# An attention and ternary-FFN kernel: strip 0's scores in the shared buffer, eight of ten transposes moved behind the second score pass

## The chip, the cores and the metric

The kernel runs on all 8 cores of one Trainium2 chip. The batch has 8 sequences, and each core computes one of them by itself with the same program. The metric is the device time of the slowest core in microseconds. One program launch does everything.

## The reference

For each sequence x of 4096 rows by 1024 columns the reference computes two residual layers:

```
x = x + attn(layernorm(x))      # f = ln(x) @ W.T + b
                                # e = f @ f.T + 0.01 * clip(|i - j|, 0, 10)
                                # a = softmax(e, rows) @ f
x = x + ffn(layernorm(x))       # scale = max(mean(|weight|), 1e-5)
                                # ternary = clip(round(weight / scale), -1, 1)
                                # ln(x) @ (ternary * scale).T
```

The score matrix e is 4096 by 4096 for each sequence. Its queries, keys and values are all the same matrix f.

## The kernel before, in words

The 4096 rows are cut into 32 strips of 128. Each engine has a queue of its own, and executes it strictly in the order in which the Python code calls `PR.add`; semaphores join the queues. All instructions of VectorE and ScalarE are recorded at line 114, a helper that wraps each call, so in the trace they are told apart by their tiles.

Phase 1 (strips 0 to 31) loads x, normalizes it, transposes it on TensorE and multiplies by W (L576). The result is `fT`, f transposed, in bf16, for all of the sequence. TensorE also transposes `fT` back into `f`, a strip at a time. The code calls that step "1c": eight 128 by 128 transposes (L481) into one of two PSUM windows `pbt`, and then one copy of 128x1024 out of the window, by VectorE or ScalarE. The two windows alternate, so the third 1c in a row waits until the first has been copied out. Eight of the 32 1c steps are done among the last groups of L576.

The FFN weight is quantized on VectorE. It lies as float32 in eight chunks (0 to 7) in `wstage`, and two instructions turn each chunk into a chunk of `wqT`. `wstage` shares its memory with three buffers of phase 2: chunks 0 to 3 lie where the scores `e` go, chunks 4 and 5 where `pT` goes, and chunks 6 and 7 where `p` goes.

Phase 2 works on one strip of 128 query rows at a time. For strip s, in the program's names:

- `emit_e_mms(s)`: the score pass, 64 matmuls of 128x512 (L723) in eight groups of eight. The groups use four PSUM banks in turn, twice (h = 0, then h = 1). A group of h = 1 waits until the group of h = 0 in its bank has been copied out.
- `emit_e_evacs(s)`: eight copies on ScalarE from PSUM to `e`, and on VectorE the distance bias and eight row maxima, then the maximum of those.
- `emit_exp(s)`: the softmax exponential on ScalarE, from `e` to `p`, with the row sum.
- `emit_A_pack(s, g)`: four packs of eight transposes that turn `p` into `pT`, each with one copy on VectorE. Except for strip 0 they stand inside the score pass of the next strip.
- the A pass: 64 matmuls of 128x512 (L953) that multiply `pT` by `f`, then residual, second layernorm, FFN (L1022) and store.

TensorE's order at the joint of the two phases is: the last L576 groups, the score pass of strip 0, ten 1c steps (`pop_1c(10)`), the score pass of strip 1, the remaining 14 1c steps, the four packs of strip 0, the A pass of strip 0, the score pass of strip 2, and so on. Of the ten 1c steps the 1st, 3rd, 5th, 7th and 9th are copied out by ScalarE, the other five by VectorE; the 14 later ones are all copied out by VectorE.

VectorE's order there is: the quantization of chunks 0 to 3, the row maxima of strip 0, the sum of four partial row sums, the quantization of chunks 4 to 7, the five 1c copies, the 14 1c copies, the four `pT` copies, the row maxima of strip 1. ScalarE's order is: the eight score copies of strip 0, its exponential, the five 1c copies, the eight score copies of strip 1, its exponential.

In the kernel before, strip 0 doesn't use `e` and `p`. Its scores go to four other buffers (`xbuf0`, `xbuf1`, `out1a`, `outbuf`), its exponentials to `lnbuf0`, `lnbuf1`, `ln2` and `ln2T`, in four instructions of 128x1024. So strip 0 doesn't wait for the quantization, and the x loads of the A passes of strips 0 and 1, which go to `xbuf0` and `xbuf1`, wait for its exponential.

Of the kernel before, what the change touches and what calls it, by code (L numbers as in the profile page):

```python
# [8 lines left out]
AF = mybir.ActivationFunctionType  # L9
ALU = mybir.AluOpType  # L10
AXX = mybir.AxisListType.X

P = 128
D = 1024
NH = D // P
# [104 lines left out]
def build_nc(S, sim_mode=False):  # L120
    NST = S // P
    HALF = S // 2
    NSH = NST // 2
    KW = min(512, HALF)
    NKB = HALF // KW
# [69 lines left out]
    with contextlib.ExitStack() as ctx:  # L195
        pb = [ctx.enter_context(nc.psum_tensor(f"pb{i}", [P, 512], F32))
              for i in range(6)]
# [16 lines left out]
        e_sb = view("e", S, F32)  # L214
        pT_sb = view("pT", S, BF16)
        p_sb = view("p", S, BF16)
        xb = [view("xbuf0", D, F32), view("xbuf1", D, F32)]
        lnb = [view("lnbuf0", D, BF16), view("lnbuf1", D, BF16)]
        out1 = [view("out1a", D, F32), view("out1b", D, F32)]
        outb = view("outbuf", D, F32)  # L220
        xb4 = xb + [out1[0], outb]
        sqscr = view("sqscr", D, BF16)
        ln2 = view("ln2", D, BF16)
        ln2T = view("ln2T", D, BF16)
# [3 lines left out]
        stats = view("stats", 48, F32)  # L228
# [6 lines left out]
        LSUM0, LSUM1, RL, SCALE, HTH, NHTH, ABSP, TOT = range(16, 24)  # L235
        PM0 = 24
        NMAX0, NMAX1, ROWI, ROWB = 32, 33, 34, 35
        ABS8 = 40

        def st_(c):  # L240
            return stats[:, c:c + 1]
# [16 lines left out]
        s_vo = mksem("svo")  # L258
# [5 lines left out]
        s_sx = mksem("ssx")  # L264
# [10 lines left out]
        PR = Prog()  # L275
# [127 lines left out]
        def emit_quant_c(c):  # L403
            def v_q(eng, c=c):
                eng.tensor_single_scalar(wqT[:, c * D:(c + 1) * D],
                                         wstage[:, c * D:(c + 1) * D],
                                         st_(NHTH), ALU.is_lt)
                return eng.scalar_tensor_tensor(
                    wqT[:, c * D:(c + 1) * D],
                    wstage[:, c * D:(c + 1) * D], st_(HTH),  # L410
                    wqT[:, c * D:(c + 1) * D], ALU.is_gt, ALU.subtract)
            waits = [(s_ss, wprep["cast_last"])] \
                if not wprep.get("quant_first") else []
            done = PR.add("vector", v_q, waits=waits, inc=s_vq)
            wprep["quant_first"] = True
            if c == 3:
                wprep["quant_e"] = done
            if c == 7:
                wprep["quant_p"] = done
                wprep["quant_last"] = done  # L420

        def x_load(k, waits, nbuf=2):
# [262 lines left out]
            nall += 1  # L685
        f_ready_ve = s_ve.v
        emit_qpre()
        for c in range(4):
            emit_quant_c(c)

        e_evac = {}
# [1 line left out]
        exp_done = {}  # L693
# [37 lines left out]
                        if hc == NH - 1:  # L731
                            e_mm_stop[(s, h, kb)] = v

        e0alt = [xb4[0], xb4[1], out1[0], outb]
        palt = [lnb[0], lnb[1], ln2, ln2T]

        def e_ap(s, bi, r0, r1):
            if s > 0:
                lo = (bi // NKB) * HALF + (bi % NKB) * KW
                return e_sb[:, lo + r0:lo + r1]  # L740
            return e0alt[bi // 2][:, (bi % 2) * KW + r0:(bi % 2) * KW + r1]

        def emit_e_evacs(s):
            c0 = max(s * P - (MAXD - 1), 0)
            c1 = min(s * P + P + MAXD - 1, S)
            for h in range(2):
                for kb in range(NKB):
                    bi = h * NKB + kb
                    lo = h * HALF + kb * KW
                    hi = lo + KW  # L750
                    bc0 = max(lo, c0)
                    bc1 = min(hi, c1)
                    wts = [(s_t, e_mm_stop[(s, h, kb)])]
                    if s > 0 and h == 0 and kb == 0:
                        wts.append((s_sx, exp_done[s - 1]))
                    if s == 1 and h == 0 and kb == 0:
                        wts.append((s_vq, wprep["quant_e"]))

                    def s_ec(eng, s=s, kb=kb, bi=bi):
                        return eng.copy(e_ap(s, bi, 0, KW), pb[kb][:, 0:KW])  # L760
                    got = PR.add("scalar", s_ec, waits=wts, inc=s_ve)
                    assert got == e_evac[(s, h, kb)], "evac reservation"

                    def v_pm(eng, s=s, lo=lo, hi=hi, bc0=bc0, bc1=bc1,
                             bi=bi):
                        if bc1 > bc0:
                            u0 = bc0 - (s * P - (MAXD - 1))
                            eng.tensor_tensor(
                                e_ap(s, bi, bc0 - lo, bc1 - lo),
                                e_ap(s, bi, bc0 - lo, bc1 - lo),  # L770
                                band[:, u0:u0 + (bc1 - bc0)], ALU.add)
                        return eng.reduce_max(st_(PM0 + bi),
                                              e_ap(s, bi, 0, KW), AXX)
                    PR.add("vector", v_pm,
                           waits=[(s_ve, e_evac[(s, h, kb)])], inc=s_vmax)

            def v_max(eng, s=s):
                return eng.reduce_max(st_(NMAX0 + s % 2),
                                      stats[:, PM0:PM0 + 2 * NKB], AXX,
                                      negate=True)  # L780
            max_done[s] = PR.add("vector", v_max, inc=s_vmax)

        def emit_exp(s):
            sc_w = [(s_vmax, max_done[s])]
            if s == 1:
                sc_w.append((s_vq, wprep["quant_p"]))
            if s > 0:
                sc_w.append((s_t, A_done[s - 1]))

            if s == 0:  # L790
                nch = S // D

                def s_exp0(eng):
                    inst = None
                    for j in range(nch):
                        inst = eng.activation(
                            palt[j][:, 0:D], e0alt[j][:, 0:D], AF.Exp,
                            bias=st_(NMAX0), scale=1.0,
                            accum_out=st_(ABS8 + 4 + j))
                    return inst  # L800
                exp_done[s] = PR.add("scalar", s_exp0, waits=sc_w, inc=s_sx)

                def v_lsum(eng):
                    return eng.reduce_sum(st_(LSUM0),
                                          stats[:, ABS8 + 4:ABS8 + 4 + nch],
                                          AXX)
                PR.add("vector", v_lsum, waits=[(s_sx, exp_done[s])],
                       inc=s_vo)
                return

            def s_exp(eng, s=s):
                return eng.activation(p_sb[:, 0:S], e_sb[:, 0:S], AF.Exp,
                                      bias=st_(NMAX0 + s % 2), scale=1.0,
                                      accum_out=st_(LSUM0 + s % 2))
            exp_done[s] = PR.add("scalar", s_exp, waits=sc_w, inc=s_sx)
# [3 lines left out]
        emit_e_mms(0, h_waits=[e0_h0, f_ready_ve])  # L819
        emit_e_evacs(0)  # L820
        emit_exp(0)
        for c in range(4, NH):
            emit_quant_c(c)

        all_1c = c1_half0 + list(range(NSH, NST))
# [2 lines left out]
        def pop_1c(n, eng=None):  # L828
            for _ in range(n):
                if not all_1c:  # L830
                    return
                stt = all_1c.pop(0)
                fw = None
                if stt >= NSH and onec_state[0]:
                    fw = (s_ve, f_ready_ve)
                    onec_state[0] = False
                i = onec_state[1]
                onec_state[1] += 1
                emit_1c(stt, fw, evac_eng=eng or
                        ("scalar" if i % 2 == 0 else "vector"))  # L840

        pop_1c(10)
        f_done = [(s_vp, s_vp.v), (s_sp2, s_sp2.v)]

        NJT = NST
# [5 lines left out]
        for s in range(NST + 1):  # L851
            live = s < NST
            def emit_A_pack(s, g):
                j0 = 8 * g
                n = min(8, NJT - j0)
                if s == 0:
                    srcs = [palt[(j0 + j) // (D // P)][
                        :, ((j0 + j) % (D // P)) * P:
                        ((j0 + j) % (D // P) + 1) * P] for j in range(n)]
                else:  # L860
                    srcs = [p_sb[:, (j0 + j) * P:(j0 + j + 1) * P]
                            for j in range(n)]
                dst = pT_sb[:, j0 * P:(j0 + n) * P]
                transpose_pack(srcs, dst,
                               extra_waits=[(s_sx, exp_done[s])])
                pT_evac[(s, g)] = s_vp.v
# [67 lines left out]
            if live:  # L934
# [31 lines left out]
                    xw = [(s_vln, ln_done[NST - 1])]  # L966
                else:
                    xw = [(s_vo, out1_done[s - 2])]
                if s <= 1:
                    xw.append((s_sx, exp_done[0]))  # L970
                xl = x_load(NST + s, xw)

                out1_nb = {}
# [128 lines left out]
```

How the kernel before makes its waits and increments, by code:

```python
    def emit(self, eng_obj, name, guard_sem=None):  # L52
        guard = None
        if guard_sem is not None:
            guard = _ChainGuard(eng_obj, guard_sem)
            eng_obj = guard
        waited = {}
        for fn, waits, inc, inc_amt, post in self.streams[name]:
            for (s, v) in waits:
                if waited.get(s.name, -1) >= v:
                    continue
                waited[s.name] = v
                eng_obj.wait_ge(s.h, v)
            inst = fn(eng_obj)
            if inc is not None:
                assert inst is not None
                if guard is not None and inc_amt != 16:
                    guard.commit_group(inst, inc, post)
                else:
                    inst.then_inc(inc.h, inc_amt)
# [15 lines left out]
    def _flush_prev(self):  # L86
        if self._prev is not None:
            self._prev.then_inc(self._sem.h, 1)
            self._n += 1
            self._marker = (self._sem.h, self._n)
            self._prev = None
# [1 line left out]
    def commit_group(self, inst, inc, post_val):  # L93
        assert inst is self._prev or self._prev is None
        self._prev = None
        inst.then_inc(inc.h, 1)
        self._marker = (inc.h, post_val)
# [1 line left out]
    def wait_ge(self, *a, **k):  # L99
        return self._eng.wait_ge(*a, **k)
# [9 lines left out]
        def wrap(*a, **k):  # L110
            self._flush_prev()
            if self._marker is not None:
                self._eng.wait_ge(self._marker[0], self._marker[1])
            inst = real(*a, **k)
            self._prev = inst
            return inst
```

## Time and profile before

| what | value |
|---|---|
| median of three runs | 1306.87 us (1306.41 to 1306.93) |
| the profiled execution's own time | 1306.79 us |
| span of its slowest core, core 0 | 1305.0 us |
| spans of the other seven cores | 1300.9 to 1303.0 us |
| TensorE matmul busy | 1247.5 us, 96% |
| VectorE busy | 610.7 us, 47% |
| ScalarE busy | 446.4 us, 34% |
| mean granted TensorE clock, by core | 0.986 to 0.989 |

The span is the time from a core's first to its last instruction. Times in the rows are counted from the span's start. A clock of 1.00 in a row is the full 2.4 GHz of TensorE, 0.50 is 1.2 GHz, and a value between is a mean over the stretch.

### The profile page before, as it was taken

The page shows a single profiled execution, that of the slowest core. Times are in us where ns is not written, and L with a number is a line of the kernel's source. Part 1 is how long each engine was busy: PE and PEld are TensorE (multiplying, and loading weights), DVE is VectorE, ACT ScalarE, POOL GpSimd, SP SyncE. Part 2 cuts the span into 40 slices and gives each one's busy share as a digit, 9 for nine tenths or more (in the row PEclk, how much of TensorE's full clock was granted, in tenths as well). Part 3 has the DMA queues.
Part 4 walks back from the last instruction along what each step waited for, and adds up shares of the span by engine and source line. Part 5 has one row for each costly group of instructions (what it writes and reads, how often), then busy time and mean ns, then how long its engine had stood idle before and what let it go on. Part 6 is the DMA issues. An engine that isn't in the chain of part 4 may idle for free.

```text
span 1305.0 us, 19556 instructions; the slowest of 8 cores (1300.9 to 1305.0 us)
## 1 busy us (share of the span) xinstructions
PE 1247.5 (96%) x7100; PEld 632.2 (48%) x7100; DVE 610.7 (47%) x945; ACT 446.4 (34%) x670; POOL 12.6 (1%) x29
## 2 busy tenths in 40 slices
PE   4999976899999999999999999999999999999986
PEld 4544444544444444444444444444444444444454
DVE  4666643644444444444444444444444444444442
ACT  5676652122333333333333322222233333333310
POOL 1000000000000000000000000000000000000000
PEclk9999997999999999999999999999999999999998
DMA  9643100000001001110010001000010110100100
GB/s 289 207 122 125 33 1 33 1 17 26 25 32 33 33 33 33 33 33 33 33 33 33 33 33 33 33 33 33 33 33 33 33 33 33 33 33 33 33 33 33
DMA packets 16254, 59.98 MB, mean 46 GB/s; under 512 B 1824, under 2 KB 1824, under 8 KB 16160
## 3 DMA queue, kind: packets, MB, share of 16 engines
q1 hardware_dynamic: 12096, 44.05, 10.2%
q0 software_dynamic: 2912, 10.49, 2.5%
q10 hardware_dynamic: 1152, 4.19, 1.0%
q8 instruction: 58, 0.95, 0.3%
q14 instruction: 36, 0.29, 0.1%
HBM read 41.95 MB, written 16.78 MB: 45 GB/s over the span
## 4 chain that ended last, share of the span: by engine, by line
PE 93%; DVE 3%; DMA 2%; issue 1%; ACT 1%; POOL 0%; DVEq 0%; ACTq 0%; POOLq 0%
PE pb L723 34%; PE pb L953 34%; PE pb L1022 8%; PE pb L576 8%; PE pbt L481 7%; DMA wtstage<-wt 2%; PE pb L336 1%; DVE f L114 1%; DVE wqT L114 1%; DVE stats L114 0%; DVE outbuf L114 0%; ACT lnbuf L114 0%; DVE lnbuf L114 0%; DVE pT L114 0%; ACT fT L114 0%
## 5 line engine op out<-in xcount | busy, mean ns | idle before, releaser
L723 PE MATMUL pb<-fT 128*128 128x512 bf16 x2048 | 467.8, 380 | 0.5 <-ACT fT L114 0.5
L953 PE MATMUL pb<-f,pT 128*128 128x512 bf16 x2048 | 447.2, 379 | 0.0
L953 PEld LDWEIGHTS pb<-f,pT 128*128 128x128 bf16 x2048 | 199.0, 98 | 234.1
L723 PEld LDWEIGHTS pb<-fT 128*128 128x128 bf16 x2048 | 195.5, 98 | 214.3 <-issue 2.0
L114 ACT COPY e<-pb 128x512 f32<-128x512 f32 x248 | 145.6, 587 | 197.5 <-PE pb L723 189.6
L114 ACT ACTIVATE p<-e,stats 128x4096 bf16<-128x4096 f32 x31 | 115.1, 3711 | 258.8 <-DVE stats L114 258.8
L114 DVE TENSOR_REDUCE stats<-e 128x1 f32<-128x512 f32 x248 | 170.2, 686 | 27.1 <-DVE stats L114 1.8
L114 DVE COPY pT<-pbt 128x1024 bf16<-128x1024 bf16 x128 | 88.5, 692 | 102.9 <-PE pbt L481 98.6
L1022 PE MATMUL pb<-wqT,ln2T 128*128 128x512 bf16 x512 | 115.7, 379 | 1.0 <-DVE ln2T L114 1.0
L114 DVE COPY ln2T<-pbt 128x1024 bf16<-128x1024 bf16 x32 | 22.1, 692 | 182.2 <-PE pbt L481 182.2
L481 PEld LDWEIGHTS pbt<-id,p 128*128 128x128 bf16 x992 | 66.3, 99 | 32.2 <-issue 3.6
L1022 PEld LDWEIGHTS pb<-wqT,ln2T 128*128 128x128 bf16 x512 | 50.0, 98 | 61.3 <-issue 1.3
L481 PE MATMUL pbt<-id,p 128*128 128x128 bf16 x992 | 76.1, 220 | 3.5 <-DVE pT L114 3.5
L114 ACT ACTIVATE sqscr<-out1a,stats 128x1024 bf16<-128x1024 f32 x24 | 27.6, 1151 | 137.8 <-DVE stats L114 137.0
L114 ACT ACTIVATE sqscr<-out1b,stats 128x1024 bf16<-128x1024 f32 x15 | 17.3, 1151 | 133.4 <-DVE stats L114 133.4
L114 DVE SCALAR_TENSOR_TENSOR out1b<-pb,stats,xbuf 128x512 f32<-128x512 f32 x32 | 24.0, 751 | 79.0 <-PE pb L953 77.0
L114 DVE SCALAR_TENSOR_TENSOR out1a<-pb,stats,xbuf 128x512 f32<-128x512 f32 x32 | 24.0, 751 | 78.0 <-PE pb L953 76.4
L576 PE MATMUL pb<-ln1Tr,WT 128*128 128x512 bf16 x256 | 58.4, 379 | 0.0
L576 PE MATMUL pb<-ln1T,WT 128*128 128x512 bf16 x256 | 57.9, 379 | 0.0
L114 ACT ACTIVATE fT<-pb,b_sb 128x512 bf16<-128x512 f32 x64 | 44.1, 688 | 34.4 <-PE pb L576 30.1
L114 DVE SCALAR_TENSOR_TENSOR outbuf<-pb,stats,out1b 128x512 f32<-128x512 f32 x32 | 24.0, 751 | 47.2 <-PE pb L1022 45.6
L114 DVE SCALAR_TENSOR_TENSOR outbuf<-pb,stats,out1a 128x512 f32<-128x512 f32 x32 | 24.0, 751 | 44.8 <-PE pb L1022 43.1
(77 smaller groups left out, 576.7 us busy)
## 6 DMA issues: line engine op xcount, KB each, us to landing
xbuf<-x SPq DMA_DIRECT2D x42, 512.0 KB, 4.3
out<-outbuf SPq DMA_DIRECT2D x32, 512.0 KB, 2.9
out1a<-x SPq DMA_DIRECT2D x8, 512.0 KB, 3.9
xbuf<-x POOLq DMA_DIRECT2D x6, 512.0 KB, 3.9
outbuf<-x POOLq DMA_DIRECT2D x6, 512.0 KB, 3.9
wtstage<-wt ACTq DMA_DIRECT2D x4, 512.0 KB, 13.5
wtstage<-wt POOLq DMA_DIRECT2D x4, 512.0 KB, 17.7
wstage<-ft POOLq DMA_DIRECT2D x4, 512.0 KB, 27.1
```

The source lines that it names most:

```text
L114: inst = real(*a, **k)
L336: inst = eng.matmul(pb[bank][:, 0:P], ones_sb[:, 0:P], ones_sb[:, 0:P], start=True, stop=True)
L481: inst = eng.transpose(win[:, t * P:(t + 1) * P], s, id_sb[:, 0:P])
L576: inst = eng.matmul(pb[pair + nb][:, 0:kw], WT[:, dc * D + hc * P:dc * D + (hc + 1) * P], lnt[:, base + nb * kw:base + (nb + 1) * kw], sta ...
L723: return eng.matmul(pb[kb][:, 0:KW], fT[:, hc * S + s * P:hc * S + (s + 1) * P], fT[:, hc * S + h * HALF + kb * KW: hc * S + h * HALF + (k ...
L953: return eng.matmul(fw_ps[nb], pT_sb[:, jt * P:(jt + 1) * P], f_sb[:, jt * D + nb * 512: jt * D + (nb + 1) * 512], start=(jt == 0), stop=( ...
L1022: inst = eng.matmul(fw_ps[nb], ln2T[:, ic * P:(ic + 1) * P], wqT[:, ic * D + nb * 512: ic * D + (nb + 1) * 512], start=(ic == 0), stop=(ic ...
```

## The change

Strip 0 uses `e` and `p` as all other strips do: its scores are copied to `e`, one instruction makes the exponential and its row sum, and the four partial sums and the instruction that adds them are gone. As chunks 0 to 3 lie under `e`, strip 0's first score copy now waits for their quantization (`quant_e`), and as chunks 6 and 7 lie under `p`, its exponential waits for theirs (`quant_p`). The quantization of chunks 6 and 7 is moved ahead of the row maxima of strip 0 on VectorE; that of chunks 4 and 5 stays behind them. The two x loads no longer wait for strip 0's exponential. And only two 1c steps stand between the score passes of strips 0 and 1 instead of ten; the other eight are done behind the score pass of strip 1, where `pop_1c(99, eng="vector")` now does 22 with copies on VectorE.

```diff
             if c == 7:
                 wprep["quant_p"] = done
+            if c == 5:
                 wprep["quant_last"] = done
...
         emit_qpre()
-        for c in range(4):
+        for c in (0, 1, 2, 3, 6, 7):
             emit_quant_c(c)
...
-        e0alt = [xb4[0], xb4[1], out1[0], outb]
-        palt = [lnb[0], lnb[1], ln2, ln2T]
-
-        def e_ap(s, bi, r0, r1):
...
-                    if s == 1 and h == 0 and kb == 0:
+                    if s == 0 and h == 0 and kb == 0:
                         wts.append((s_vq, wprep["quant_e"]))
 
-                    def s_ec(eng, s=s, kb=kb, bi=bi):
-                        return eng.copy(e_ap(s, bi, 0, KW), pb[kb][:, 0:KW])
+                    def s_ec(eng, kb=kb, lo=lo, hi=hi):
+                        return eng.copy(e_sb[:, lo:hi], pb[kb][:, 0:KW])
...
             sc_w = [(s_vmax, max_done[s])]
-            if s == 1:
+            if s == 0:
                 sc_w.append((s_vq, wprep["quant_p"]))
             if s > 0:
                 sc_w.append((s_t, A_done[s - 1]))
-
-            if s == 0:
-                nch = S // D
-
-                def s_exp0(eng):
-                    inst = None
-                    for j in range(nch):
-                        inst = eng.activation(
-                            palt[j][:, 0:D], e0alt[j][:, 0:D], AF.Exp,
-                            bias=st_(NMAX0), scale=1.0,
-                            accum_out=st_(ABS8 + 4 + j))
-                    return inst
-                exp_done[s] = PR.add("scalar", s_exp0, waits=sc_w, inc=s_sx)
...
-        for c in range(4, NH):
+        for c in (4, 5):
             emit_quant_c(c)
...
-        pop_1c(10)
+        pop_1c(2)
...
-                if s == 0:
-                    srcs = [palt[(j0 + j) // (D // P)][
-                        :, ((j0 + j) % (D // P)) * P:
-                        ((j0 + j) % (D // P) + 1) * P] for j in range(n)]
-                else:
-                    srcs = [p_sb[:, (j0 + j) * P:(j0 + j + 1) * P]
-                            for j in range(n)]
+                srcs = [p_sb[:, (j0 + j) * P:(j0 + j + 1) * P]
+                        for j in range(n)]
...
-                if s <= 1:
-                    xw.append((s_sx, exp_done[0]))
                 xl = x_load(NST + s, xw)
```

## Rows read from the trace of the kernel before

**Rows 1.** The page: busy time of the engines over core 0's span.
```profile
PE 1247.5 (96%) x7100; PEld 632.2 (48%) x7100; DVE 610.7 (47%) x945; ACT 446.4 (34%) x670; POOL 12.6 (1%) x29
```
**Rows 2.** Windows, core 0: stretch, length, busy PE PEld DVE ACT POOL, clock, DMA share, GB/s.
```profile
36.00:154.00 118.00, 113.80 (x678) 55.76 (x677) 78.36 (x109) 81.78 (x162) 6.37 (x12) 0.99 0.41 126
...
316.00:1116.00 800.00, 800.00 (x4420) 391.96 (x4418) 356.58 (x564) 244.50 (x337) 0.00 (x0) 1.00 0.10 32
```
**Rows 3.** Timeline, core 0, TensorE from strip 0's score pass: start, duration, what.
```profile
174.41 13.97 PE L723 MATMUL pb<-fT 128*128 128x512 bf16 x64 [0.54 <-ACT fT L114]
...
188.22 1.06 PE L481 MATMUL pbt<-id,fT 128*128 128x128 bf16 x16
...
196.90 1.01 PE L481 MATMUL pbt<-id,fT 128*128 128x128 bf16 x8 [7.63 <-ACT f L114]
...
205.90 1.86 PE L481 MATMUL pbt<-id,fT 128*128 128x128 bf16 x16 [8.00 <-DVE f L114]
```
**Rows 4.** Timeline, core 0, from strip 1's score pass to strip 0's A pass.
```profile
213.08 14.91 PE L723 MATMUL pb<-fT 128*128 128x512 bf16 x64
...
227.83 1.06 PE L481 MATMUL pbt<-id,fT 128*128 128x128 bf16 x16
...
228.61 11.20 DVE L114 COPY f<-pbt 128x1024 bf16<-128x1024 bf16 x14 [14.46 <-PE pbt L481]
...
242.13 13.98 PE L953 MATMUL pb<-f,pT 128*128 128x512 bf16 x64
```
**Rows 5.** Timeline, core 0, VectorE and ScalarE between the two score passes.
```profile
189.28 0.69 DVE L114 TENSOR_REDUCE stats<-outbuf 128x1 f32<-128x512 f32 x1 [1.04 <-ACT outbuf L114]
...
190.39 1.15 ACT L114 ACTIVATE lnbuf<-xbuf,stats 128x1024 bf16<-128x1024 f32 x1 [1.27 <-DVE stats L114]
...
195.73 1.03 ACT L114 ACTIVATE f<-pbt 128x1024 bf16<-128x1024 bf16 x1
...
205.06 0.69 DVE L114 COPY f<-pbt 128x1024 bf16<-128x1024 bf16 x1
```
**Rows 6.** Timeline, core 0, VectorE and ScalarE around strip 0's first scores.
```profile
168.36 0.75 DVE L114 TENSOR_SCALAR wqT<-wstage,stats 128x1024 bf16<-128x1024 f32 x1
...
175.98 1.28 DVE L114 SCALAR_TENSOR_TENSOR wqT<-wstage,stats,wqT 128x1024 bf16<-128x1024 f32 x1
176.44 0.59 ACT L114 COPY xbuf<-pb 128x512 f32<-128x512 f32 x1 [1.06 <-PE pb L723]
```
**Rows 7.** Timeline, core 0, row maxima and exponential of strip 1.
```profile
243.68 6.21 DVE L114 TENSOR_REDUCE stats<-e 128x1 f32<-128x512 f32 x8
...
250.42 3.71 ACT L114 ACTIVATE p<-e,stats 128x4096 bf16<-128x4096 f32 x1 [21.70 <-DVE stats L114]
```
**Rows 8.** The chain that ended last, core 0: start, duration, what.
```profile
257.83 0.45 PE pbt L481 x8
```
**Rows 9.** Windows, core 0, two short stretches, columns as in the second group.
```profile
194.00:196.00 2.00, 0.00 (x0) 0.00 (x0) 0.16 (x1) 1.81 (x5) 0.00 (x0) 0.62 0.00 0
...
228.00:242.00 14.00, 10.29 (x142) 7.99 (x140) 11.40 (x17) 0.59 (x1) 0.00 (x0) 1.00 0.00 1
```
**Rows 10.** Windows, core 6, one short stretch, columns as in the second group.
```profile
209.00:212.00 3.00, 2.14 (x31) 1.79 (x29) 0.97 (x2) 1.37 (x2) 0.00 (x0) 0.92 0.00 0
```
**Rows 11.** Timeline, core 6, TensorE from its longest stand to its second score pass.
```profile
205.38 1.86 PE L481 MATMUL pbt<-id,fT 128*128 128x128 bf16 x16 [8.00 <-DVE f L114]
...
211.79 2.54 PE L723 MATMUL pb<-fT 128*128 128x512 bf16 x11
```
**Rows 12.** Span and mean granted clock of the second slowest core.
```profile
core 6: 1303.0 us, clock 0.988
```
**Rows 13.** Timeline, core 1, TensorE: strip 0's score pass and its A pass.
```profile
172.72 13.97 PE L723 MATMUL pb<-fT 128*128 128x512 bf16 x64 [0.54 <-ACT fT L114]
...
238.73 13.98 PE L953 MATMUL pb<-f,pT 128*128 128x512 bf16 x64
```
**Rows 14.** The page, DMA issues: queue, count, size, median us to landing.
```profile
xbuf<-x SPq DMA_DIRECT2D x42, 512.0 KB, 4.3
```

More of the change, by code:

```diff
@@ L732, in emit_e_mms @@
                             e_mm_stop[(s, h, kb)] = v
-        e0alt = [xb4[0], xb4[1], out1[0], outb]
-        palt = [lnb[0], lnb[1], ln2, ln2T]
-        def e_ap(s, bi, r0, r1):
[L738 to L741, printed above, removed]
         def emit_e_evacs(s):
@@ L768, in v_pm @@
                             eng.tensor_tensor(
-                                e_ap(s, bi, bc0 - lo, bc1 - lo),
-                                e_ap(s, bi, bc0 - lo, bc1 - lo),
+                                e_sb[:, bc0:bc1], e_sb[:, bc0:bc1],
                                 band[:, u0:u0 + (bc1 - bc0)], ALU.add)
-                        return eng.reduce_max(st_(PM0 + bi),
-                                              e_ap(s, bi, 0, KW), AXX)
+                        return eng.reduce_max(st_(PM0 + bi), e_sb[:, lo:hi],
+                                              AXX)
                     PR.add("vector", v_pm,
@@ L788, in emit_exp @@
                 sc_w.append((s_t, A_done[s - 1]))
-            if s == 0:
-                nch = S // D
-                def s_exp0(eng):
-                    inst = None
-                    for j in range(nch):
-                        inst = eng.activation(
-                            palt[j][:, 0:D], e0alt[j][:, 0:D], AF.Exp,
-                            bias=st_(NMAX0), scale=1.0,
-                            accum_out=st_(ABS8 + 4 + j))
-                    return inst
-                exp_done[s] = PR.add("scalar", s_exp0, waits=sc_w, inc=s_sx)
[L803 to L809, printed above, removed]
             def s_exp(eng, s=s):
```

## The prediction, made before the change was run

> **What bounds the kernel now.** I read the page first. TensorE is busy 1247.5 us of 1305.0 [rows 1], so a change can only gain where TensorE stands still or is slow. Two long windows say where that is not: over 316 to 1116 us TensorE is busy 800.00 of 800.00 us, at clock 1.00, and before the joint of the phases, from 36 to 154 us, 113.80 of 118.00 us [rows 2]. The long middle has no slack that could swallow a gain or a loss made ahead of it: whatever moves the start of strip 0's A pass moves the end by as much.
>
> Then the timeline around the change. Strip 0's score pass runs from 174.41 us, and TensorE's next work, the first two 1c steps, starts at 188.22 [rows 3]. After them it stands 7.63 us, does one 1c step, stands 8.00 us, and goes on in pieces [rows 3]; strip 1's score pass begins only at 213.08 [rows 4]. That is 24.86 us (213.08 − 188.22) for ten 1c steps.
>
> The reader is to see why in the two engines that empty the windows. The third 1c step needs the window of the first, whose copy stands in ScalarE's queue behind strip 0's exponential: that starts at 190.39, the copy at 195.73 [rows 5]. The fourth needs the window of the second, whose copy stands in VectorE's queue behind the quantization of chunks 4 to 7, and starts at 205.06 [rows 5]. The score pass of strip 1, which needs neither window, is queued on TensorE behind all this. During the pause the clock falls, within 194 to 196 us (mean 0.62) [rows 9], so the second pass starts at 1.2 GHz: it takes 14.75 us to the next instruction's start (227.83 − 213.08) against 13.81 (188.22 − 174.41) for the first [rows 3, 4].
>
> **The 1c steps.** With two 1c steps there, both windows are free and nothing is waited for. Eight back-to-back transposes advance TensorE's queue by 0.45 us [rows 8], so strip 1's score pass can start at 188.22 + 0.90 = 189.12. Term one: 213.08 − 189.12 = **23.96 us gained**. Its banks: the four groups of h = 0 need the h = 1 copies of strip 0, the last of which ends before the row maximum at 189.28 [rows 5], while bank 3 is not wanted before 189.12 + 3 × 1.73 = 194.3 (1.73 is 13.81/8). No wait.
>
> **The second half of strip 1's pass.** The group h = 1 of bank 0 would start at 189.12 + 6.91 = 196.03. It needs strip 1's first score copy, which on ScalarE stands behind the exponential and one 1c copy. The single exponential takes 3.71 us [rows 7]; the four took 1.15 each, but 5.34 / 4 = 1.335 to the next instruction's start (195.73 − 190.39) [rows 5], so 0.18 comes on top, and the 1c copy starts at 190.39 + 3.89 = 194.28. Its 1.03 us [rows 5] end at 195.31; the score copy, 0.59 us [rows 6], starts some 0.1 later and ends near 196.0. With some 0.1 for the signal (an estimate from the 0.13 us between the end of a 1c copy at 205.75 and the transposes at 205.90 [rows 3, 5]) TensorE resumes near 196.17: a stall of 0.1 to 0.2 us, and I take 0.14. Later groups are 1.73 us apart and their copies 0.7 (0.59 and some 0.1 between) [rows 6]: no further wait. The pass runs at full clock, as TensorE hasn't paused: 13.81 + 0.14 = 13.95. Term two: 14.75 − 13.95 = **0.80 gained**.
>
> **Eight more 1c steps behind it.** There they are paced by VectorE: 14 copies fill 11.20 us, 0.80 each [rows 4]. 22 copies take 17.60. Term three: 8 × 0.80 = **6.40 lost**. The lead-in (0.78 us from transpose to first copy) and the way out (2.32 us from the end of the last 1c copy, 239.81, to the A pass at 242.13, with four packs) stay [rows 4].
>
> Check by the absolute times: 189.12 + 13.95 + 0.78 + 17.60 + 2.32 = 223.77 for the A pass, against 242.13.
>
> **Strip 0 in `e` and `p`.** The new wait of the first score copy is for chunk 3, whose second instruction ends at 177.26 (175.98 + 1.28); the copy started at 176.44 before, so it comes some 0.95 later [rows 6]. It ends at 178.0. Behind it stand seven copies, 0.7 us each where the groups come each 1.73: the second is back in step within 0.1 us. TensorE first wants that bank at 174.41 + 6.91 = 181.3, so 3.3 us cover it.
>
> Chunks 6 and 7 now stand ahead of the row maxima. Four chunks took from 168.36 to 177.26, with the gap behind each 2.25 [rows 6], so the maxima start at 181.9 instead of 177.4. With 0.4 for the bias and 0.79 for each of seven maxima (eight in 6.21, plus the gap to the next) [rows 7] the backlog ends at 187.8. The eighth has to wait for its data until 189.28 anyway [rows 5]. Cover 1.5 us; the exponential still starts at 190.39, and its own new wait (chunk 7, 181.87) is long met. Without that cover each microsecond would delay exponential and score copy, and so TensorE, by as much. Chunks 4 and 5 take 4.5 us from about 190.4 and are followed by one 1c copy, done by 195.7, while TensorE wants that window at 203. The one exponential ends 1.45 us sooner than the four (5.34 − 3.89); term two contains that.
>
> **The x loads** are released about 45 us sooner, at strip 31's layernorm, on SyncE's queue, where only the first stores stand behind them. A load lands in 4.3 us [rows 14], and the A pass's end is 80 us off: nothing either way.
>
> **The sum.** 23.96 + 0.80 − 6.40 = **18.36 us gained** on core 0: span 1305.0 − 18.4 = 1286.6. The profiled execution's own time is 1306.79, 1.79 above its span and 0.08 below the median of the runs. 1306.87 − 18.4 = **1288.5 us**.
>
> The other cores gain less. Core 1's A pass, at 238.73, would move to 172.72 + 49.36 = 222.08 (49.36 = 223.77 − 174.41, core 0's new distance), 16.65 gained [rows 13]. With the same on core 6, its span becomes 1303.0 − 16.65 = 1286.4 [rows 12], close under core 0's 1286.6, so core 0 still sets the end. If core 0 gained only 16.7 too, the time would be 1290.2.
>
> **A rule against it.** The new order has a stretch of nothing but transposes, 22 + 4 packs, 20.8 us long (26 × 0.80). In the trace 14 + 4 packs kept the clock at 1.00 through 228 to 242 us [rows 9], and on core 6 the clock rose to a mean of 0.92 within 209 to 212 us, while from 205.38 on nothing but transposes had run up to 211.79 [rows 10, 11]. The Trainium skill, "TensorE: Matmul & The Clock Gate", section Part 4 on the PE-mode transpose, says that transposes don't count as busy for the clock in the same way, and that full clock doesn't engage for them. By that rule the clock would drop inside the longer stretch, and the time would be that of rival 1, 1292 instead of 1288.5; the rows here speak against it.
>
> **Rival 1, the clock drops among the transposes.** On core 0 it fell at about 194.5, 6.3 us after the last dense matmul (188.2). If transposes kept nothing up, it would fall at 203.1 + 6.3 = 209.4; about 19 packs would follow at 0.93 us (1.86 for two at 1.2 GHz) [rows 3] instead of 0.80, 2.5 us, and the A pass would start slow: 0.94 as the pass of term two did, or 3.6 if, as before, 7.2 us of work (205.90 to 213.08) went by at half clock first. 1291.9 to 1294.6; near the low end, as dense matmuls begin at once, **1292**. For it: the stretch is longer than any shown. Against: both rows above. Chance 0.06.
>
> **Rival 2, the wait comes back on ScalarE or VectorE.** If the exponential started or ran later (a backlog of row maxima over its cover of 1.5 us, or 5.34 us as the four exponentials took instead of 3.89), strip 1's second half would stall, each microsecond in full, by 1 to 2 us: **1290**. It would also cover a core 0 that gains only as much as core 1. Chance 0.10.
>
> **Rival 3, no gain.** The change wouldn't do what it says if TensorE's wait only moved: the new first wait would have to be 18 us long at 196. ScalarE's queue holds 5.7 us in all between the last maximum and the copy, so I see no work that could fill it. 1306.9, chance 0.02.
>
> **Rival 4, slower than before.** The pause may be what keeps the clock full later: with it gone, all cores run dense matmuls from 36 us on without a rest. The price is in the 1063 us from the A pass: at a mean clock of 0.97 there, 33 us, and **1321** in all; it decides from a clock below 0.983, where the loss passes 18.4 us. Against it: 800 us without any idle time at 1.00, and 118 us at 0.99 before the pause [rows 2]. The Trainium skill, "TensorE: Matmul & The Clock Gate", Part 1, states a limit of 13/16 of the clock once three cores of a die run dense matmuls; with eight cores dense this trace shows 1.00 instead. Chance 0.03.
>
> **How the numbers follow.** The forecast has 0.79. Its own range is 1287.3 to 1290.3 (stall of 0 to 0.5 us, the slow start's 0.9, run to run 0.3, another core setting the end). The range 1286.5 to 1293.0 takes in rival 2 and most of rival 1, and leaves out about 0.1. A difference of 0.2%, 2.6 us, is what a measurement can tell from none here. Faster 0.95, same 0.02, slower 0.03.
>
> **What would show it.** The after trace should have the second score pass starting 14.7 us behind the first, one exponential of 3.71 us on `e` starting 16 us behind the first pass, a stall under 0.5 us in the middle of the second pass, 22 copies of 0.80 us, clock 1.00 throughout, and the A pass 49.4 us behind the first pass's start. A gap of microseconds between TensorE's two passes, slower copies, or a clock under 1.00 from 209 us on would make the prediction wrong.

## The result, and the profile after

The changed kernel takes 1287.4 us, the median of five executions (1287.3 to 1288.6), against 1306.6 us, the median of seven of the kernel before. The ratio is 0.9854, 95% interval 0.9841 to 0.9867. Executions in which one die ran at a lower granted clock than the other are left out, here and in all medians below; only the profile of "four windows, both engines" is of such an execution, and what is said of it goes by the other die. The forecast was 1288.5 us, in a range of 1286.5 to 1293.0; it was right.

The profiled execution took 1287.4 us. Its slowest core is now core 3. Spans and granted clocks of three cores:

```profile
core 0: 1284.8 us, clock 0.995
...
core 1: 1282.5 us, clock 0.997
...
core 3: 1285.7 us, clock 0.994
```

The timeline of core 3, the same pieces as in [rows 3, 4]: first score pass, two 1c steps, second score pass, the 22 steps behind it with VectorE's copies, the A pass.

```profile
173.33 13.97 PE L724 MATMUL pb<-fT 128*128 128x512 bf16 x64 [0.54 <-ACT fT L114]
...
187.14 1.06 PE L482 MATMUL pbt<-id,fT 128*128 128x128 bf16 x16
...
188.03 14.14 PE L724 MATMUL pb<-fT 128*128 128x512 bf16 x64
...
202.00 1.06 PE L482 MATMUL pbt<-id,fT 128*128 128x128 bf16 x16
...
202.79 17.68 DVE L114 COPY f<-pbt 128x1024 bf16<-128x1024 bf16 x22 [8.33 <-PE pbt L482]
...
222.78 13.98 PE L918 MATMUL pb<-f,pT 128*128 128x512 bf16 x64
```

The reader is to see one number: the distance from the start of the first score pass to the start of the A pass, 222.78 − 173.33 = 49.45 us. On core 0 before it was 67.72, on core 1 66.01 [rows 3, 4, 13]. The two stands of 7.63 and 8.00 us are gone: the second pass starts 14.70 us behind the first, 0.89 behind the first 1c step. I call this number the distance from here on. It is nearly the same on all cores of a run (49.45 to 49.68 here), while the start of the first pass itself differs by core and execution (171.9 to 174.1 us in this one), and that moves the time by 1 to 2 us between kernels that don't differ there. So the experiments are read by the distance first. What lies behind the A pass's start didn't move on the core that sets the time: 1305.0 − 242.13 = 1062.87 us before, 1285.7 − 222.78 = 1062.92 after.

VectorE and ScalarE between the passes, same core, against [rows 5, 6]:

```profile
176.34 0.59 ACT L114 COPY e<-pb 128x512 f32<-128x512 f32 x1 [2.04 <-DVE wqT L114]
...
186.47 0.69 DVE L114 TENSOR_REDUCE stats<-e 128x1 f32<-128x512 f32 x1 [0.58 <-ACT e L114]
...
188.20 0.69 DVE L114 TENSOR_REDUCE stats<-e 128x1 f32<-128x512 f32 x1 [1.04 <-ACT e L114]
...
189.36 3.71 ACT L114 ACTIVATE p<-e,stats 128x4096 bf16<-128x4096 f32 x1 [1.33 <-DVE stats L114]
...
193.26 1.02 ACT L114 ACTIVATE f<-pbt 128x1024 bf16<-128x1024 bf16 x1
193.76 0.69 DVE L114 COPY f<-pbt 128x1024 bf16<-128x1024 bf16 x1
194.37 2.61 ACT L114 COPY e<-pb 128x512 f32<-128x512 f32 x4
```

The last row maximum still waits 1.04 us for ScalarE's copy, as before [rows 5], and the seventh already waited 0.58: the backlog of chunks 6 and 7 is gone by then. The exponential is one instruction of 3.71 us, and the copy of the first 1c step starts 3.90 us behind it (predicted 3.89).

The clock, in windows of core 3 with the columns of [rows 2]:

```profile
188.00:202.00 14.00, 14.00 (x68) 6.21 (x66) 5.62 (x7) 8.97 (x11) 0.00 (x0) 1.00 0.00 1
202.00:223.00 21.00, 15.67 (x210) 12.08 (x209) 17.28 (x25) 0.59 (x1) 0.00 (x0) 1.00 0.00 1
...
316.00:1116.00 800.00, 800.00 (x4420) 391.98 (x4419) 356.54 (x564) 243.68 (x337) 0.00 (x0) 1.00 0.10 32
```

It stayed at 1.00, 2.4 GHz, through the 21 us of nothing but transposes, where the rule weighed in the prediction would have it fall.

### The profile page after: what moved, and what is told of

Same layout as the page of the kernel before. It is cut to its first block, busy times and chain, and to the rows that moved or that the text cites. A ratio compares the mean times of both kernels' runs of the same rounds, so it can differ in the third digit from the quotient of the medians.

```text
span 1285.7 us, 19544 instructions; the slowest of 8 cores (1282.5 to 1285.7 us)
## 1 busy us (share of the span) xinstructions
PE 1242.9 (97%) x7100; PEld 627.9 (49%) x7100; DVE 613.3 (48%) x948; ACT 440.5 (34%) x660; POOL 12.6 (1%) x29
## 4 chain that ended last, share of the span: by engine, by line
PE 94%; DVE 2%; DMA 2%; issue 1%; ACT 0%; POOL 0%; DVEq 0%; ACTq 0%; POOLq 0%
PE pb L724 34%; PE pb L918 34%; PE pb L985 9%; PE pb L577 8%; PE pbt L482 7%; DMA wtstage<-wt 2%; PE pb L336 1%; DVE f L114 1%; DVE stats L114 0%; DVE outbuf L114 0%; DVE lnbuf L114 0%; DVE pT L114 0%; ACT fT L114 0%; POOL wtstage L103 0%; ACT sqscr L114 0%
## 5 line engine op out<-in xcount | busy, mean ns | idle before, releaser
L114 ACT COPY e<-pb 128x512 f32<-128x512 f32 x256 | 150.2, 587 | 199.8 <-PE pb L724 189.5
L114 ACT ACTIVATE p<-e,stats 128x4096 bf16<-128x4096 f32 x32 | 118.7, 3709 | 267.5 <-DVE stats L114 267.5
L114 DVE TENSOR_REDUCE stats<-e 128x1 f32<-128x512 f32 x256 | 175.7, 686 | 28.6 <-ACT e L114 1.6
L577 PE MATMUL pb<-ln1T,WT 128*128 128x512 bf16 x256 | 57.9, 379 | 0.0
## 6 DMA issues: line engine op xcount, KB each, us to landing
wtstage<-wt POOLq DMA_DIRECT2D x4, 512.0 KB, 18.2
```

What stands on the lines that cost most here:

```text
L114: inst = real(*a, **k)
L577: inst = eng.matmul(pb[pair + nb][:, 0:kw], WT[:, dc * D + hc * P:dc * D + (hc + 1) * P], lnt[:, base + nb * kw:base + (nb + 1) * kw], sta ...
```

## The experiments

Where a ratio is given, the time is a median of three or four executions; "no 1c step" has two, "the transposes twice" and "four windows, VectorE alone" have one. The diffs are shortened, and their comments are mine. The kernel before was measured beside them each time, at 1307.0, 1307.3 and 1305.7 us (the last beside "the sum moved", "strip 0's packs inside" and "nine steps spread"), so medians of different groups can differ by 1.6 us through that alone; the ratio takes it out.

**The order alone.** Two 1c steps between the passes instead of ten, on the kernel before.

```diff
-        pop_1c(10)
+        pop_1c(2)
```

> The kernel before with two 1c steps between the score passes instead of ten, and nothing else (strip 0 stays in its own four buffers). My theory: the gain comes from the order on TensorE. The second pass starts 14.7 us behind the first, but the four exponentials take 5.34 us where one takes 3.89, so ScalarE's first score copy of strip 1 comes later and TensorE stalls about 1.5 us in the middle of the second pass (0.16 with the whole change). The A pass starts 50.8 us behind the first pass (49.45 with the whole change): 1288.8 us. Rival, the buffers and the order of the quantization carry the gain: near 1300 us or above.

Measured: 1291.5 us, ratio 0.9880 (0.9865 to 0.9895), distance 51.44 on most cores. The order alone gives most of the gain. Core 1, TensorE and VectorE:

```profile
187.51 7.07 PE L723 MATMUL pb<-fT 128*128 128x512 bf16 x32
...
194.20 0.16 DVE L114 TENSOR_REDUCE stats<-stats 128x1 f32<-128x4 f32 x1 [5.56 <-ACT ln2T L114]
...
195.96 7.07 PE L723 MATMUL pb<-fT 128*128 128x512 bf16 x32 [1.38 <-ACT e L114]
...
203.46 4.72 DVE L114 COPY f<-pbt 128x1024 bf16<-128x1024 bf16 x6
```

The second half was due at 187.51 + 6.91 = 194.42 and came at 195.96: a stall of 1.54 us, as expected. But the distance was 0.6 us above what I expected. The rows show a wait that I had overlooked: the sum of the four partial row sums (194.20) stands ahead of chunks 4 to 7 and waits 5.56 us for the exponentials, so the copy of the second 1c step starts only at 203.46, behind the end of the pass. As for the time, 1291.5 is 4.1 above the changed kernel for a distance only 2.0 longer; the first pass started up to 175.7 us in this execution, and that is the other 2.

**The sum moved.** One more edit on that kernel, to try the explanation.

```diff
-        emit_exp(0)
+        v_lsum0 = emit_exp(0)
         for c in range(4, NH):
             emit_quant_c(c)
+        PR.add("vector", v_lsum0, waits=[(s_sx, exp_done[0])], inc=s_vo)
```

> The run that changed the order alone, with one more edit: the instruction that adds the four partial row sums stands behind the quantization of chunks 4 to 7 instead of ahead of it. In the run before it, the sum held the quantization back until the four exponentials were done, and with it the copy of the second 1c step, which began 30.6 us behind the first pass's start, when TensorE already wanted that window. My theory: with the sum out of the way that copy comes at about 25 us, and the A pass at 50.85 us as I first expected, instead of 51.44: 1290.9 us. Rival, the 0.6 us come from elsewhere: still 51.4 us.

Measured: distance 50.84, 1290.1 us, ratio 0.9886 (0.9870 to 0.9903). VectorE of core 1:

```profile
196.93 0.16 DVE L114 TENSOR_REDUCE stats<-stats 128x1 f32<-128x4 f32 x1
197.19 0.69 DVE L114 COPY f<-pbt 128x1024 bf16<-128x1024 bf16 x1
...
202.84 5.55 DVE L114 COPY f<-pbt 128x1024 bf16<-128x1024 bf16 x7 [4.96 <-PE pbt L481]
```

The copy comes at 197.19, 25.2 us behind the first pass's start, and TensorE waits for nothing there. The explanation holds, by the distance: it fell by 0.60 us on the same cores. The ratio can't show it (0.9880 and 0.9886, with intervals that overlap). The change removes this wait too, since strip 0 no longer has partial sums. What is left, 50.84 − 49.45 = 1.39 us, is the difference of the two stalls in the second pass, 1.54 and 0.16, so the gain over the order alone is accounted for.

**The buffers and the quantization alone.** The changed kernel with ten steps between the passes.

```diff
-        pop_1c(2)
+        pop_1c(10)
```

> The changed kernel with ten 1c steps between the score passes, as before: only the buffers and the order of the quantization are changed. My theory: the third 1c step still waits for the copy of the first behind the exponential (until 21.0 us behind the first pass's start), but the fourth no longer waits for chunks 6 and 7, so the second pass starts 27.6 us behind the first (38.7 before), or up to 29.5 if the clock falls in the pause of 6 us. A pass at 55.7 to 57.5 us: 1293.7 to 1295.5 us. So each part alone would give most of its gain, and they don't add. Rival, the order of the 1c steps is all that counts: 1306 us.

Measured: 1296.5 us, ratio 0.9918 (0.9903 to 0.9932), distance 56.7 to 57.9 (59.1 on one core). The time is 1.0 us above the upper end of what I expected. A stand is left, and the clock falls in it, on all eight cores; on core 5, the one with 59.1, it came back only 2.6 us into the second pass. Timeline and a window of core 4:

```profile
197.74 1.87 PE L482 MATMUL pbt<-id,fT 128*128 128x128 bf16 x16 [6.23 <-ACT f L114]
```
```profile
198.00:202.00 4.00, 3.47 (x32) 2.97 (x29) 0.69 (x1) 1.79 (x2) 0.00 (x0) 0.50 0.02 4
```

So this half alone gives about 10 us, the order alone 15, both 19. They aren't additive, as each removes part of the same two waits. In distance, from the 66.0 us of core 1 before: 8.7 (to the median core's 57.3), 14.6 and 16.6 us.

**No 1c step between the passes.**

```diff
-        pop_1c(2)
+        pop_1c(0)
```

> The changed kernel with no 1c step between the score passes and all 24 behind the second, copied by VectorE. My theory: two more copies of 0.80 us in the stretch that VectorE paces (1.61), 0.89 less ahead of the second pass, and the 0.16 us stall of the second pass gone, as ScalarE has no 1c copy ahead of its score copies. A pass 50.0 us behind the first pass instead of 49.45: 1287.9 us, 0.5 above the changed kernel. Rival, fewer steps between the passes are always better: below 1287.

Measured: distance 50.01, 1288.4 us (two executions). The 24 copies of core 3:

```profile
200.37 19.30 DVE L114 COPY f<-pbt 128x1024 bf16<-128x1024 bf16 x24 [8.08 <-PE pbt L482]
```

19.30 / 24 = 0.804 each. Two is better than none, by 0.56 us of distance: two windows take two steps without any wait. Other numbers between two and ten weren't tried.

**Chunks 4 and 5 also ahead of the row maxima.**

```diff
-        for c in (0, 1, 2, 3, 6, 7):
+        for c in (0, 1, 2, 3, 6, 7, 4, 5):
             emit_quant_c(c)
...
-        for c in (4, 5):
-            emit_quant_c(c)
```

> The changed kernel with chunks 4 and 5 too quantized ahead of strip 0's row maxima. It tests the cover of 1.5 us that the prediction gave the maxima. My theory: VectorE reaches the maxima 4.5 us later, the backlog outlasts the cover by 3.1 us, and the exponential, strip 1's first score copy and the second half of strip 1's pass come 3.1 us later: stall 3.3 instead of 0.16 us, A pass at 52.6 us, 1290.5 us. Rival, the delay is hidden somewhere: 1287.4 us.

Measured: 1293.3 us, ratio 0.9893 (0.9879 to 0.9908). The distance was 52.82 on cores 1 and 7, near the 52.6 expected, but 54.4 to 54.7 on the six others. Timeline and a window of core 4:

```profile
194.53 3.71 ACT L114 ACTIVATE p<-e,stats 128x4096 bf16<-128x4096 f32 x1 [4.71 <-DVE stats L114]
...
200.26 8.75 PE L724 MATMUL pb<-fT 128*128 128x512 bf16 x31 [3.38 <-ACT e L114]
```
```profile
202.00:204.00 2.00, 2.00 (x6) 0.73 (x5) 0.00 (x0) 0.40 (x2) 0.00 (x0) 0.51 0.00 0
```

The same stand on core 7:

```profile
183.80 1.28 DVE L114 SCALAR_TENSOR_TENSOR wqT<-wstage,stats,wqT 128x1024 bf16<-128x1024 f32 x1 [0.46 <-DVE wqT L114]
...
200.27 5.99 PE L724 MATMUL pb<-fT 128*128 128x512 bf16 x27 [3.37 <-ACT e L114]
```

The cover was as short as predicted: each microsecond beyond it arrived on TensorE. The 0.3 us above the expected delay is a gap between two quantization instructions (0.46 us where 0.1 is usual, first line above), whose cause stays open. On six cores the clock also fell to 1.2 GHz for a while, in the stand or up to 1.1 us behind it, and that cost another 1.6 to 1.7 us that I had not priced (cores 2 and 4, at 54.7, reach the second pass 0.22 us later in the changed kernel too); on the two others the same stand left it at 1.00.

**The transposes twice.** Each of the last 22 steps is done a second time, so this is added work with the same result.

```diff
                     pop_1c(99, eng="vector")
+                    for stt in range(NST - 22, NST):
+                        emit_1c(stt, None, evac_eng="vector")
```

> The changed kernel with the last 22 1c steps done a second time behind the first 22, with the same operands, so 44 copies and the four packs of strip 0 stand between dense matmuls, some 39 us of nothing but transposes. It tests the rule against the change. My theory: transposes keep the clock up; the added steps cost 22 times 0.804, 17.7 us, clock 1.00 throughout, A pass at 67.1 us: 1305.1 us. Rival, the clock falls in the longer stretch: rows below 1.00 behind 209 us, packs of 0.93 instead of 0.80 us, and a slow start of the A pass: 1308 to 1312 us.

Measured: 1307.0 us, distance 67.64. The copies on core 3, and a window over them:

```profile
202.60 24.15 DVE L114 COPY f<-pbt 128x1024 bf16<-128x1024 bf16 x30 [8.33 <-PE pbt L482]
227.25 11.20 DVE L114 COPY f<-pbt 128x1024 bf16<-128x1024 bf16 x14 [0.50 <-DVE f L114]
```
```profile
202.00:242.00 40.00, 29.84 (x390) 22.55 (x388) 33.29 (x49) 0.59 (x1) 0.00 (x0) 1.00 0.01 1
```

Clock 1.00 over 40 us of transposes, on all eight cores. The 0.5 us of distance above my figure is one gap behind the 30th copy, whose cause stays open. The time is 1.9 above it; the slowest core, core 0, also began its first pass at 175.6 us.

**Two engines over two windows.** The 22 copies alternate between ScalarE and VectorE.

```diff
-                    pop_1c(99, eng="vector")
+                    emit_e_evacs(1, "copy")   # strip 1's score copies first
+                    pop_1c(99)
```

> The changed kernel with the 22 1c copies alternating between ScalarE and VectorE, over the same two windows (ScalarE's score copies of strip 1 are put ahead of them in its queue, which changes nothing else). My theory: with two windows the pair is bound by ScalarE's window: 0.79 us from the transposes to the copy, 1.03 for the copy and 0.13 for the signal, 1.95 us for two packs, 0.975 each instead of 0.804. A pass at 53.2 us: 1291.2 us, 3.8 slower than the changed kernel. Rival, the copies are bound by VectorE's work alone, and half the work elsewhere speeds them up: below 1285.

Measured: 1293.7 us, ratio 0.9891 (0.9873 to 0.9909), distance 53.1 to 54.1. Timeline and a window of core 2:

```profile
206.60 1.02 ACT L114 ACTIVATE f<-pbt 128x1024 bf16<-128x1024 bf16 x1 [0.90 <-PE pbt L482]
...
207.77 1.05 PE L482 MATMUL pbt<-id,fT 128*128 128x128 bf16 x16 [0.87 <-ACT f L114]
208.53 1.02 ACT L114 ACTIVATE f<-pbt 128x1024 bf16<-128x1024 bf16 x1 [0.90 <-PE pbt L482]
```
```profile
226.00:229.00 3.00, 2.84 (x25) 2.25 (x23) 2.12 (x4) 0.00 (x0) 0.00 (x0) 0.50 0.02 5
```

And a window of core 6:

```profile
207.00:210.00 3.00, 2.53 (x25) 2.30 (x23) 0.69 (x1) 1.02 (x1) 0.00 (x0) 0.50 0.00 0
```

Two packs take 1.93 us, the cycle of ScalarE's window, and both copying engines wait. Cores 5 and 7, where the clock stayed at 1.00, have the expected distance, 53.1. On five of the eight cores the clock fell to 1.2 GHz for a while: on cores 1, 2 and 3 at strip 0's packs, but on cores 4 and 6 only 4.3 and 4.1 us after the transposes began, with no stand over 1.15 us before. That cost 0.5 to 0.8 us of distance.

**Four windows, VectorE alone.** The two PSUM banks of the A pass, idle then, become windows.

```diff
-        twb = [pbt[0][:, 0:1024], pbt[1][:, 0:1024]]
+        twb = [pbt[0][:, 0:1024], pbt[1][:, 0:1024],
+               pb[4][:, 0:512].bitcast(BF16), pb[5][:, 0:512].bitcast(BF16)]
...
-                    pop_1c(99, eng="vector")
+                    for k, stt in enumerate(all_1c):   # 22 steps
+                        emit_1c(stt, fw, evac_eng="vector", wsel=k % 4)
```

> The changed kernel with four windows (the two pbt and the two idle banks of the A pass) for the 22 1c steps, all still copied by VectorE. My theory: VectorE's copies already follow each other without a gap, 0.80 us each, so more windows give nothing: A pass at 49.4 us, 1287.4 us. Rival, the hand-over of the two windows is part of the 0.80: the pitch falls to the 0.70 of one copy, A pass at 47.2 us, 1285.2 us.

Measured: 1289.0 us, distance 49.6 to 50.0. Timeline and two windows of core 2:

```profile
207.90 1.49 DVE L114 COPY f<-pbt 128x1024 bf16<-128x1024 bf16 x2
```
```profile
219.67:221.55 1.88, 0.00 (x1) 0.03 (x1) 1.57 (x4) 0.00 (x0) 0.00 (x0) 1.00 0.00 0
...
223.00:226.00 3.00, 2.83 (x19) 2.11 (x20) 2.10 (x4) 0.00 (x0) 0.00 (x0) 0.50 0.00 0
```

The copies keep a pitch of 0.79 us: VectorE itself is the bound, not the windows. TensorE runs ahead as far as its four windows allow. But strip 0's packs use only the first two windows, as before, so TensorE stands 1.88 us until VectorE has emptied the first of them, and the clock falls behind it. The pitch is shown; the distance of 49.6 to 50.0 contains this fall, and the time is of one execution.

**Four windows, both engines.** Of five copies VectorE takes three and ScalarE two.

```diff
-                        emit_1c(stt, fw, evac_eng="vector", wsel=k % 4)
+                        emit_1c(stt, fw, evac_eng="vsvvs"[k % 5] == "v"
+                                and "vector" or "scalar", wsel=k % 4)
```

> Four windows and both engines: of five copies VectorE takes three (0.80 us each) and ScalarE two (about 1.13 each with the gap), so 0.48 us per pack; TensorE needs 0.45. My theory: A pass at 14.7 + 13.97 + 0.78 + 22 times 0.48 + 2.32 = 42.4 us behind the first pass, 1280.4 us, 7 us faster than the changed kernel. Rival, one of the two alone is what counts: no faster than the better of the two runs before it (four windows alone, two engines alone).

Measured: 1282.2 us, ratio 0.9807 (0.9790 to 0.9825), distance 43.22 on core 3. Neither half had helped alone; together they give 6.2 us of distance. It is 0.8 above my figure; packs and A pass of core 3:

```profile
213.57 1.02 ACT L114 ACTIVATE f<-pbt 128x1024 bf16<-128x1024 bf16 x1
214.12 1.23 PE L486 MATMUL pbt<-id,p 128*128 128x128 bf16 x16 [0.74 <-DVE f L114]
...
214.90 3.10 DVE L114 COPY pT<-pbt 128x1024 bf16<-128x1024 bf16 x4 [1.03 <-PE pbt L486]
...
216.97 2.32 PE L937 MATMUL pb<-f,pT 128*128 128x512 bf16 x10
```

At the hand-over to strip 0's packs TensorE waits 0.74 us for a window, and VectorE stands 1.03 us before their first copy. My sum had no wait there.

**Strip 0's packs inside the second pass, on top of that.**

```diff
-                if s > 0:
-                    pre = {k + 1: (lambda s=s, g=k: emit_A_pack(s, g))
-                           for k in range(npack)}
-                else:
-                    pre = None
+                k0 = 1 if s > 0 else 4
+                pre = {k + k0: (lambda s=s, g=k: emit_A_pack(s, g))
+                       for k in range(npack)}
```

> The kernel with four windows and both engines, with strip 0's four packs moved inside the second half of strip 1's score pass, as for all other strips. My theory: TensorE pays 4 times 0.45 for them in the pass instead of 2.85 us behind the last 1c step, and then waits about 0.5 us more for the last ScalarE copy: A pass at 42.8 us instead of 43.2, 1281.8 us. Rival, the packs' copies weren't on the path: no change, 1282.2.

Measured: distance 42.63, 1281.4 us, ratio 0.9819 (0.9802 to 0.9835). Core 3:

```profile
215.21 1.02 ACT L114 ACTIVATE f<-pbt 128x1024 bf16<-128x1024 bf16 x1
...
216.38 3.83 PE L933 MATMUL pb<-f,pT 128*128 128x512 bf16 x17 [1.36 <-ACT f L114]
```

The A pass now waits for the last ScalarE copy alone. This is the shortest distance that I found, 0.59 below the run before; by the ratios (0.9819 and 0.9807) the times can't be told apart.

**Nine steps spread into the second pass.** Nine 1c steps stand between its last groups, and the other 13 are mixed with the packs behind it.

```diff
+                    pre = {5: lambda: more(3, (0, 1, 2), (V, V, V)),
+                           6: lambda: more(3, (3, 0, 1), (V, V, V)),
+                           7: lambda: more(3, (2, 3, 0), (V, V, V))}
...
+                    seq = "svAsvAsvAsvAsvsvs"   # s, v: a 1c step by that engine
```

> The kernel with four windows and both engines, with nine 1c steps moved between the last groups of strip 1's score pass (0.45 us of TensorE each, copies by VectorE, which is idle there), and behind the pass the other 13 and strip 0's four packs mixed, ten copies by VectorE (8.0 us) and seven or fewer by ScalarE. My theory: A pass at 14.7 + 13.97 + 4.05 + 8.95 = 41.7 us, 1280.7 us. Rival, TensorE's own 0.45 us per pack is already the bound in the run before: no gain, 1282.2 us. TensorE's floor for the passes and 28 packs is 27.6 + 12.6 = 40.2 us.

Measured: 1283.4 us, ratio 0.9831 (0.9814 to 0.9847), distance 43.06 where I expected 41.7. The end on core 3:

```profile
213.48 1.02 ACT L114 ACTIVATE f<-pbt 128x1024 bf16<-128x1024 bf16 x1 [0.57 <-PE pbt L486]
...
214.60 1.02 ACT L114 ACTIVATE f<-pb 128x1024 bf16<-128x1024 bf16 x1
...
215.71 1.02 ACT L114 ACTIVATE f<-pbt 128x1024 bf16<-128x1024 bf16 x1
...
216.88 2.32 PE L952 MATMUL pb<-f,pT 128*128 128x512 bf16 x10 [1.51 <-ACT f L114]
```

The miss lies in the sequence: the nine steps cost the pass their 4.05 us, as expected (it ends 18.0 us behind its start), but I gave ScalarE three of the last five copies, and with 1.12 us each they end alone and the A pass stands 1.51 us. A sequence that ends on VectorE wasn't tried. By the ratio this run, too, can't be told from the two before it.

## Why the prediction was right

**Term one, the waits ahead of the second pass.** Predicted start 14.71 us behind the first pass, measured 14.70. The order alone showed the same start, so it is TensorE's order that removes both stands.

**Term two, the second pass.** Predicted 13.95 us, measured 202.00 − 188.03 = 13.97. With four exponentials the stall became 1.54 us, and with the exponential 3.4 us late it grew by 3.4, to 3.5: the chain maximum, exponential, 1c copy, score copy was the right one. (The 0.13 us that the prediction read off for the signal is 0.15 by its own two times, 205.75 and 205.90; that changes nothing.) The 0.80 us of this term were there to gain on core 0 alone. On the seven other cores of the kernel before the clock was back at 1.00 ahead of the second pass, which took 13.8 us already, as on core 3:

```profile
211.39 13.98 PE L723 MATMUL pb<-fT 128*128 128x512 bf16 x64
...
225.21 1.06 PE L481 MATMUL pbt<-id,fT 128*128 128x128 bf16 x16
```

**Term three, eight more copies.** Predicted 17.60 us for 22 copies, measured 17.68. With 24 the distance grew by 0.56, with 44 by 18.2.

**The covers.** The predicted cover of 1.5 us can be read in the trace after: the seventh and eighth maxima waited 0.58 + 1.04 = 1.62 us for their data, less the 0.1 between two maxima. With 4 and 5 as well the end moved by the part above it. For rival 2 the prediction priced such a stall at its own length; where the clock fell with it, it cost 1.6 to 1.7 us more.

**The sum.** The A pass was predicted 49.36 us behind the first pass and came at 49.45. On core 0 the distance shrank from 67.72 to 49.46, 18.26 us against 18.36 predicted. The time fell by 19.2 (1306.6 − 1287.4). The 0.9 between them lies ahead of the first score pass: the slowest core began it at 174.41 before and at 173.33 after. The change touches nothing there that I can name, and over all profiled executions that start lay between 171.6 and 176.6 us, by core and run, so I count it as scatter and not as a gain: that the time came out 1.1 us below the forecast says nothing for or against it. Nor is all of the 18.3 us the same for every core. The seven other cores gained 16.4 to 16.7 us of distance, and core 0, which set the time before, 1.7 more, because its clock came back last, at 215.0 us, 1.9 us into its second pass. Which core is hit differs between executions of the kernel before, but nearly each of them has one; the one in which no core's mean clock was under 0.988 took 1304.3 us.

**The x loads.** They were issued at 146.61 us on core 3, against 195.72 on core 0 before, and nothing behind the A pass's start changed (1062.87 and 1062.92 us), as predicted.

**The rivals.** The clock didn't fall among the transposes of the changed kernel, nor in 40 us of them. The Trainium skill, "TensorE: Matmul & The Clock Gate", Part 4, says that transposes don't count as busy in the same way; in these two runs they kept the clock at 1.00. Rival 1 stays possible for other kernels: with the packs 0.965 us apart on average (two engines over two windows) the clock did fall among them on five of eight cores. Rival 2 didn't occur; quantizing chunks 4 and 5 early shows what it would have been. Rivals 3 and 4 didn't occur either: TensorE was busy 800.00 of 800.00 us at 1.00 after the joint, as before.

## What to carry to other kernels

When an engine stands still, look at what is queued behind the instruction that waits: work that needs nothing of the late result can go ahead of it, and that alone was worth 15 of 19 us. Count how many steps the buffers take without a wait, and start with that many there: of none, two and ten, two was the shortest. Where a producer is paced by copies, try buffers and copying engines together: here four windows alone and two engines alone were both no faster, together they took 6.2 us of distance off; and check that whatever is queued ahead of a late copy (here, a small sum that waits for another engine) isn't itself waiting.

## What the runs showed of the hardware

- A stand of 3.4 us between dense matmuls made the clock fall to 1.2 GHz on six of eight cores and left it at 2.4 GHz on two, in the same execution. The fall came in the stand or up to 1.1 us behind it, and cost the six 1.6 to 1.7 us. In the kernel before the clock fell on every core, in a stand of 7.6 us. The stall of 1.5 us in the second pass (the order alone, the sum moved) left it at 1.00 on all eight.
- Transposes alone can bring the clock back: in the kernel before it returned to 2.4 GHz on seven cores 1.2 to 2.7 us ahead of the second pass, when TensorE had done nothing but transposes, with stands between them, since the first pass.
- Whether transposes hold the clock depended on how they came. With packs 0.80 us apart it stayed at 1.00 on all eight cores, for 21 and for 40 us. With two engines over two windows (two packs in each 1.93 us) it fell on five of eight cores, on two of them 4.1 and 4.3 us after the first transpose. With four windows and VectorE alone it fell on all eight, in a stand of 1.9 us or up to 1.3 us behind it, after some 16 us of transposes. No run separates the stands from the sparser packs, so the condition stays open; the prediction took more for granted than these runs show.
- A VectorE copy of 128x1024 bf16 out of PSUM keeps a pitch of 0.79 to 0.80 us with four windows as with two, 0.10 above its 0.69.
